# The first attention layer of a four-stage kernel with the operations of three batches in a new order on every engine

## The reference

```
x = x + gnn(layernorm(x), adj)                      # first stage
h = layernorm(x) @ W[head]                          # 512 x 64
weight[i,j] = leaky_relu(e_src[i] + e_dst[j], 0.01) # -1e9 where adj[i,j] == 0
attention = softmax(weight over j)
out = relu(attention @ h + bias) + h
gnn = layernorm over the 64 columns of out, * gamma + beta, heads side by side
```

## Time and profile before

| | us |
|---|---|
| median of 3 runs | 4832.03 |
| the profiled execution | 4839.06 |
| its span | 4837.3 |
| first score piece (DVE, line 847) starts | 43.69 |
| last one of the stage starts | 1216.75 |
| last operation of the stage (POOL, line 1053) starts | 1246.58 |

### The profile page before, as it was taken

The page is one execution under the profiler, slowest core; times in us unless marked ns, Lnnn a source line. Parts: engine busy times, 40 slices in busy tenths (PEclk is TensorE's granted clock), DMA queues, the critical chain, the costliest instruction groups (busy, mean ns, idle before and its releaser), DMA issues. The chain is left out here.

```text
span 4837.3 us, 142627 instructions
## 1 busy us (share of the span) xinstructions
PE 4119.1 (85%) x55809; PEld 2885.5 (60%) x55809; DVE 3534.2 (73%) x8962; ACT 2911.6 (60%) x7074; POOL 1201.2 (25%) x1028
## 2 busy tenths in 40 slices
PE   7888888888399999999998999975888888888882
PEld 4444444444156666666665788854777777777772
DVE  5888888888388888888887677753666666666666
ACT  5777777777298888888886666641333332333330
POOL 3666666665222222222222000000000000000000
PEclk9999999999699999999999999987999999999996
DMA  2121111111100000000001333331111111111115
GB/s 61 60 63 54 53 62 62 53 53 45 53 23 27 27 27 27 27 23 23 27 27 39 109 119 116 118 108 24 34 40 41 39 37 41 42 34 40 43 30 158
DMA packets 326283, 252.58 MB, mean 52 GB/s; under 512 B 171244, under 2 KB 289772, under 8 KB 323564
## 3 DMA queue, kind: packets, MB, share of 16 engines
q1 hardware_dynamic: 324076, 235.03, 16.8%
q10 hardware_dynamic: 1536, 8.39, 0.6%
HBM read 159.42 MB, written 67.11 MB: 47 GB/s over the span
## 5 line engine op out<-in xcount | busy, mean ns | idle before, releaser
L2309 PE MATMUL lstm_G_psum<-lstm_Whh,lstm_HT 128*32 128x192 f32 x8192 | 440.4, 333 | 268.1 <-DVE lstm_HT L2486 267.8
L847 DVE CUSTOM_DVE_ANT_0 g_S<-g_Z_psum,g_relu 128x512 f32<-128x512 f32 x640 | 438.3, 685 | 301.6 <-ACT g_relu L617 299.7
L617 ACT ACTIVATE g_relu<-g_Z_psum,g_src 128x512 f32<-128x512 f32 x640 | 436.8, 682 | 291.0 <-PE g_Z_psum L463 288.7
L2379 ACT ACTIVATE lstm_TC<-lstm_G_psum 128x192 f32<-128x192 f32 x512 | 170.9, 334 | 708.5 <-PE lstm_G_psum L2309 708.5
L473 PE MATMUL g_PT_psum<-g_ident,g_PR 128*128 128x128 f32 x2560 | 398.9, 279 | 158.3 <-DVE g_PT L855 92.3
L473 PEld LDWEIGHTS g_PT_psum<-g_ident,g_PR 128*128 128x128 f32 x2560 | 301.7, 142 | 354.1 <-ACT g_PR L651 237.2
L1785 ACT ACTIVATE ssm_EX<-ssm_Z_psum,ssm_tok 128x256 f32<-128x256 f32 (+1 forms) x1024 | 372.6, 424 | 155.1 <-PE ssm_Z_psum L1615 85.5
L651 ACT ACTIVATE g_PR<-g_S,g_nmax 128x512 f32<-128x512 f32 x640 | 456.9, 714 | 0.1
L2301 PE MATMUL lstm_G_psum<-lstm_Wih,lstm_XT 128*32 128x192 f32 x8192 | 428.0, 327 | 0.0
L2309 PEld LDWEIGHTS lstm_G_psum<-lstm_Whh,lstm_HT 128*32 128x32 f32 x8192 | 214.2, 109 | 355.2 <-DVE lstm_HT L2486 321.5
L2475 DVE SCALAR_TENSOR_TENSOR lstm_AB<-lstm_TC 128x128 f32<-128x128 f32 x512 | 150.2, 293 | 335.5 <-ACT lstm_TC L2379 331.5
(11 more groups left out here) (266 smaller groups left out, 10614.2 us busy)
## 6 DMA issues: line engine op xcount, KB each, us to landing
g_ADJ<-in_adj SPq DMA_DIRECT2D x64, 1024.0 KB, 5.6
x<-g_XO SPq DMA_DIRECT2D x64, 512.0 KB, 3.4
g_X<-in_x SPq DMA_DIRECT2D x32, 512.0 KB, 4.3
ssm_X<-x SPq DMA_DIRECT2D x32, 512.0 KB, 3.9
x<-ssm_OUT SPq DMA_DIRECT2D x32, 512.0 KB, 2.9
g_X<-x SPq DMA_DIRECT2D x32, 512.0 KB, 3.9
lstm_raw<-x SPq DMA_DIRECT2D x1024, 16.0 KB, 1.8
lstm_U<-x SPq DMA_DIRECT2D x128, 128.0 KB, 3.5
```

The lines of the kernel that those rows point to most:

```text
L617: act.activation(relu[n % 4][:, :], score_bank(b, n)[:, :], ACT.Relu, scale=(1.0 - ALPHA) / ALPHA, bias=src[b.slot][:, t, HH * p + hh:HH * ...
L847: v.tensor_tensor_reduce(S[n % 4][:, :], score_bank(b, n)[:, :], relu[n % 4][:, :], -1.0, 3e38, ALU.add, ALU.min, nmax[:, n % 4:n % 4 + 1] ...
L2309: ins = pe.matmul(bank[32 * j:32 * (j + 1), 0:last - first], HT[t % 2][:, 32 * kc:32 * (kc + 1)], Whh[:, kc, j, first:last], start=False, ...
```

## The change

`attention_phase(layer 0)` is replaced by a function of its own, `first_attention_phase`, which does the same operations on the same shapes. The order on each engine is no longer a loop over items but a list, `period(b)`, in which up to three batches stand beside each other, and the loop runs over periods. On DVE the list of period b has the work after the items of b-2, the items from 5 on of b-1, the first five items of b, and the statistics and first masks of b+1. `BANK` says which side bank each product uses, `DRAIN` what has read it, and `BEFORE` who had the bank before it in the list, and `bank_free` waits for that. The columns go to `Ab[1]` and stand before the projections; the outputs of the first pair of heads go to `Ab[0]`, those of the second to `Ab[1]` (both to `Ab[1]` before). POOL does the normalisation for b+2 first and the last step of the normalisation after the items one period later. `xt_out` also waits for both halves of the projections of the batch before, `relu_part` of item 0 waits for the first stage of `split` instead of the last, `h_out` also for `HB`, `load_x` also for `XN`. The statistics of batch 0 come after the preparations of the weights instead of before them.

The diff, cut to what is spoken of; of the lists of operations a few lines stand, their order shows below:

```diff
--- before.py
+++ after.py
@@ -1082,6 +1082,629 @@
+def first_attention_phase(nc, nb, x_in, adj, weights, consts, x_out, kept):
...
+    SLOTS = 3
+    NP = 2
+    ITEMS = 16
+    HH = 2
...
+        DRAIN = {"xnt0": (("xt", 2, 1),), "xnt1": (("xt", 2, 2),), "pj0": (("h", 2, 1),), "pj2": (("h", 2, 2),),
+                 "co0": (("s1", 1, 1),), "pt": (("rows", 1, 1),), "ob0": (("d1", 2, 1),), "ob1": (("d1", 2, 2),)}
+        BANK = {"xnt0": Ab[0], "xnt1": Ab[1], "pj0": Ab[0], "pj2": Ab[1], "co0": Ab[1], "pt": Ab[1], "ob0": Ab[0],
+                "ob1": Ab[1]}
+        BEFORE = {"xnt0": (("pj0", -1), ("ob0", -2),), "xnt1": (("pj2", -1), ("ob1", -2),), "pj0": (("xnt0", 0),),
+                  "pj2": (("pt", 0),), "co0": (("xnt1", 0),), "pt": (("co0", 0),), "ob0": (("pj0", 1), ("ob0", -1),),
+                  "ob1": (("pj2", 1), ("ob1", -1),)}
+        def bank_free(b, op):
+
+            for was, ago in BEFORE[op]:
+                if 0 <= (b + ago).off < nb:
+                    for sem, per, count in DRAIN[was]:
+                        (b + ago).wait(nc.tensor, s[sem], per, count)
...
+            def load_x(b):
+                if b.off == 0:
+                    return
+                b.wait(sp, s["xb"], 1, 1 - SLOTS)
+                b.wait(sp, s["xn"], IT, (1 - SLOTS) * IT)
+                sp.dma_start(X[b.slot][:, :, :], xv[b.index()]).then_inc(x_loaded[b.slot], 16)
+
+            def load_adj(b):
+                b.wait(sp, s["mask"], 1, 0)
+                b.wait(sp, s["check"], IT, 0)
+                sp.dma_start(ADJ[:, :, :], av[b.index()]).then_inc(s["adj_loaded"], 16)
+
+            def store(b):
+                b.wait(sp, s["out"], 1, 1)
+                sp.dma_start(ov[b.index()], XO[b.slot][:, :, :]).then_inc(stored[b.slot], 16)
+
+            def period(b):
+                at(b + 4, load_adj)
+                at(b + 5, load_x)
+                at(b, store)
+
+            for k in range(-5, nb + 0):
...
+            def xn_turned(b, kc):
+                b.wait(pe, s["xn"], IT, IT)
+                bank_free(b, f"xnt{kc}")
...
+            def columns(b, half_of):
+                b.wait(pe, s["xt"], 2, 2)
+                if half_of == 0:
+                    bank_free(b, "co0")
...
+            def outputs_turned(b, p):
+                b.wait(pe, s["ot"], NP, p + 1)
+                bank_free(b, f"ob{p}")
...
+            def period(b):
+                at(b, xn_turned, 0)
+                at(b + -1, scores, 9)
+                at(b + -1, turn, 6)
...
+            for k in range(0, nb + 1):
+                period(Batch(None, k, SLOTS))
...
+            def xt_out(b, kc):
+                b.wait(act, s["h_pe"], 2, 0)
+                b.wait(act, s["e_pe"], 1, 0)
+                b.wait(act, s["xt_pe"], 2, kc + 1)
...
+            def relu_part(b, n):
+                p, t, hh = item(n)
+                b.wait(act, s["z"], ITEMS, n + 1)
+                b.wait(act, s["s"], ITEMS, n - 3)
+                if n == 0:
+                    b.wait(act, s["s1"], 1, 1)
...
+                at(b, exp, 10)
+                at(b + -1, square)
...
+            def norm_stats(b):
+                b.dma_wait(v, x_loaded)
+                b.wait(v, s["xn"], IT, 0)
...
+            def normalise(b, p):
+                b.wait(v, s["ob"], NP, p + 1)
+                b.wait(v, s["rinv"], 1, 1)
+                b.wait(v, s["out"], 1, 0)
...
+                at(b + -2, residual)
+                at(b + -1, leaky, 9)
+                at(b + -2, residual_sum)
...
+            def period(b):
+                at(b + 2, normalised)
+                at(b + -1, layernorm, 3)
+                at(b + 1, bias_added)
+                at(b, centred)
+                at(b, residual)
+                at(b, layernorm, 0)
+                at(b, layernorm, 1)
+                at(b, layernorm, 2)
...
-        attention_phase(nc, 0, nb, a["x"], a["adj"], pick(GNN0), consts, x1, kept)
+        first_attention_phase(nc, nb, a["x"], a["adj"], pick(GNN0), consts, x1, kept)
```

476 lines of the change are left out of this document (added).

## The result

| | before | after |
|---|---|---|
| median, us | 4830.8 (4827.99 to 4834.06, 4 runs) | 4602.93 (4598.8 to 4605.82, 4 runs) |
| profiled execution, its span | 4839.06, 4837.3 | 4598.8, 4597.0 |
| last POOL operation of the stage ends | 1248.92 | 1015.04 |
| from there to the end of the span | 3588.4 | 3582.0 |

The ratio is 0.9527 (95% 0.9511 to 0.9544): 228 us less, where 152 were forecast and 4630 was the low end of the range. All of it is in the first stage (1248.92 less 1015.04 is 233.9); the later stages differ by 6.4, about the spread of the runs before (6.1).

The account below looks back on a forecast made before the run. A ring of waits bounds the kernel now, with no engine full; afterwards DVE's 32.3 us a period. 41.0 + 31 x 32.3 + 26 + 8.5 + 20.0 ends the stage at 1096.8, 152 earlier: 4680 us, range 4630 to 4760.

Parts of the forecast that it names:

- the low end of the range: Lowest total time the forecast range allowed: 4630 us, a first-stage period of T = 30.7 us.
- the DVE term: DVE's work per first-stage period, taken as 32.3 us with all four masks slow, and as the bound.
- The rule weighed there: Two-port VectorE operations and any GpSimd operation exclude each other for the whole instruction; so masks beside `XN` are slow.
- the rival "DVE falls to 29.3 to 30.3 and PE is the bound": First stage: masks beside `XN` are fast, PE sets T = 31.0 us, time 4640 us; chance 0.17.
- T: Period per batch in the first stage, forecast as 32.3 us and multiplied by 31 in the sum.
- tails: On PE, 0.16 us counted as busy ahead of each of some 8 waits a period, taken off its 31.40.
- The walk through the lists: DVE's list laid out over 32.3 us against the other engines: they come in time, so DVE runs without gaps.
- waits are left over: First stage: thin margins leave 2.2 us of the 5.3 us of gaps, T = 34.5, 4748 us; chance 0.25.
- no gain: First stage: the ring of waits re-forms elsewhere, T about 36.5 to 37.2, 4810 to 4832 us; chance 0.03.
- the chain over the load of `X`: Sum, centring, beta residual, load, statistics hold DVE: T = 37.2 to 37.5, 4832 to 4842 us; chance 0.05 (slower).
- The start: From weights' preparation to the first `leaky`: forecast at 41.0 us, 2.7 earlier than 43.69, with columns at 1.85.
- The square's stall: ACT's square waits 3.44 us for POOL, delaying a relu and DVE by 2.23 us; forecast to go.

Follow-up runs that it names:

- Experiment 5: Kernel before with only the four masks moved in DVE's list from items 4, 5, 6, 8 to 7, 8, 9, 12: 4827.01 us, ratio 0.9987.
- experiment 3: Kernel after without the product that adds the mask to the scores, 16 PE products fewer a batch: 4553.54 us, ratio 0.9432.
- experiment 1: Kernel after with a batch's four masks moved in DVE's list back towards POOL's large additions: 4616.49 us, ratio 0.9558.
- experiment 6: Kernel after with the first head pair's four weigh steps in two twos instead of one by one: 4602.67 us, ratio 0.9523.
- experiment 12: Kernel after with two more `bn_stats` a batch on DVE, 0.7 us of work that nobody reads: 4613.64 us, ratio 0.9545.
- experiment 4: Kernel before with ACT's square one item later and DVE's sum of squares in item 0 of the next batch: 4786.35 us, ratio 0.9911.
- 11: Kernel before with the first head pair's turned outputs in `Ab[0]` and the second's in `Ab[1]`, order unchanged: 4843.41 us, ratio 1.0020.
- Experiment 9: Kernel before with square and squares' sum later and the masks at items 7, 8, 9, 12: 4837.64 us, ratio 1.0008.
- experiment 10: Kernel before with square and squares' sum later and the masks at items 8, 9, 10, 12: 4794.69 us, ratio 0.9922.
- experiment 8: Kernel after with statistics and normalisation of batch 0 ahead of the weights' preparation: 4593.19 us, ratio 0.9501.

## Why the prediction was wrong in size and right in kind

The stage ends 82 us earlier than forecast (1015.04 against 1096.8). By the terms of the sum:

| term | forecast | measured | difference |
|---|---|---|---|
| first `leaky` | 41.0 | 42.17 | +1.2 |
| 31 distances from batch to batch | 31 x 32.3 = 1001.3 | 26.1 + 30 x 29.8 = 920.1 | -81.2 |
| last batch's 16 items | 26 | 25.9 | -0.1 |
| last `leaky` to the end | 28.5 | 26.9 | -1.6 |

- **The step that failed** is the DVE term: "With all four slow DVE has 32.3 us of work, with three fast 29.3. I take 32.3, by the nearest rows that are masks." All four are fast, and DVE's work is 28.6 us a period, 3.7 less. The two beside `XN`, which no row of before showed, run at full speed inside it; the timeline of the kernel after:

```profile
219.10 5.09 POOL L1653 TENSOR_SCALAR g_XN<-g_X,g_mv,g_rstd 128x256 f32<-128x256 f32 x4
...
223.54 0.41 DVE L1521 TENSOR_SCALAR g_MASK<-g_ADJ 128x512 bf16<-128x512 int32 x1
```
```profile
221.52 1.22 POOL L1653 TENSOR_SCALAR g_XN<-g_X,g_mv,g_rstd 128x256 f32<-128x256 f32 x1
...
222.72 1.47 POOL L1653 TENSOR_SCALAR g_XN<-g_X,g_mv,g_rstd 128x256 f32<-128x256 f32 x1
```

The last two lines are the third and the fourth of the four operations under `XN`: the fourth, into which both masks reach, takes 0.25 longer, so here POOL pays a little, and DVE 0.1 for one mask and nothing for the other. The mask beside the last normalisation (212.27, 0.42) falls beside an operation on 16 columns, and the one ahead of `bias_added` (228.13, 0.42) between two of POOL's. The nearest row was the slow mask beside an addition, but the cast inside `XN` was the row on the operation in question. Experiment 5 shows the same in the old order, with `XN` in both.
- The rule weighed there, the Trainium skill, "SBUF — State Buffer", section "Who interferes with whom", puts every operation of GpSimd in the same lock. The trace agrees for the two-input operations of 1024 columns (0.91, 2.22, 2.25 us) and not for the `XN` normalisation, whose masks took 0.41, 0.42 and 0.51, nor for the operation on 16 columns. The measurement decides: in the runs here only masks that meet a `TENSOR_TENSOR` of 1024 columns wait.
- The window of 36.70 us from which the sum took DVE's 31.34 and PE's 31.40 was short of a full period by 0.33. In the full 37.03 DVE is busy 31.67 and PE 31.74. With three masks 1.0 shorter that gives 28.7 for DVE, and 28.6 was measured.
- **The bound.** With fast masks the rival "DVE falls to 29.3 to 30.3 and PE is the bound" is what happened: PE is the fullest engine (29.64 of 29.80), and the period falls when products are taken from it (experiment 3). With DVE at 28.6 and ACT at 28.3 behind it the bound is not PE's alone, as experiments 1, 6 and 12 show. It was sized too high, T = 31.0: PE's work was put at 30.1 to 31.4 and is at most 29.64, and of the 0.9 us of waits that I added almost none is left. The 1.3 us of tails that I took off were too few: a full period of before has PE busy 31.74, 2.1 above what the same products take in the unbroken queue. And T stood for all 31 distances, but the first one, with no work of earlier batches in it, is 26.1 (33.98 against 37.03 before). So three terms were off in one direction, which is why even the low end (T = 30.7) did not hold the time: -75 us by the 30 full periods and -6 by the first.
- **The walk through the lists held.** Square with hardly a wait (forecast 0.4, none recorded), relus early, side banks and `X` in time: DVE's only waits a period are 0.6 for a turn and 0.3 for the outputs. The rival "waits are left over" is refuted (T 34.5), as are "no gain" and the chain over the load of `X`: its load is issued at 209.72, 5.9 after the sum, and the statistics start at 215.42, 5.7 later, with no recorded wait.
- **The start** is 1.2 later: the columns took 3.55 and not 1.85 us, and what follows them was 0.5 shorter than forecast. The last batch's items were met (25.9 against 26).
- Where the gain comes from: 7.2 us a period, 37.03 to 29.80, is the closing of gaps and the shorter masks. The square's stall alone gives 1.5 (experiment 4), masks alone 0.2 (5), banks alone less than nothing (11). Inside the whole order the places of the masks are worth 14 us, the bank 18, a wrong block of weigh steps 85. So the parts do not add up one by one: most of the gain belongs to the list as a whole. How it divides over its further moves was not tried.
- Experiment 9 lost its gain to the place of one slow mask and not to the clock (the windows of experiment 10). Why a mask at item 7 costs 1.5 us a period where three slow ones at items 4 to 6 cost nothing is not shown.

## What to carry to other kernels

Where no engine is full and the waits form a ring, lay the new list out against the fullest engine's work and trust the walk, but price each operation by the row beside the same neighbour, and carry the second-fullest engine through the sum with equal care: it becomes the bound. Single fixes in a ring of waits return little (43, 6 and -9 us here, of 228), and work taken off an engine that waits returns as waiting. Once an order is tight, 0.6 or 0.7 us more on an engine that has 1.2 to spare already shows (experiments 1 and 12), and any change of a neighbour's duration or place has to be timed.

## What the hardware did that was not expected

- A mask of DVE (128x512, int32 to bf16) that starts inside a POOL `TENSOR_TENSOR` of 1024 columns ends 0.28 us after it (330.67 + 0.91 against 331.30; 199.28 + 2.22 against 201.21 is 0.29), in the one case 0.63 us ahead of that end and in the other 1.93. Beside POOL's `TENSOR_SCALAR` of 256 columns it took 0.41 and 0.51, and POOL's operation 1.47 instead of 1.22.
- The columns took 3.55 us for 16 products at the start of the kernel after and 1.85 before, with a recorded granted clock of 1.00 (2.4 GHz) in both. They stood behind 1.76 us without products now, behind 6.77 us of unbroken ones before. In the kernel of experiment 8 they take 3.55 again, also behind 1.76. It is not the columns alone: the 8 projections right behind them took 3.76 in the kernel after, where 8 take 1.99 in the earlier trace rows, and before, the 16 projections ahead of the columns took 6.77. So PE worked at half its later pace for some microseconds, in both kernels, while the record says 1.00.
- Moving three masks by an item moved the mean granted clock of the stage from 0.94 to 0.97 in the old order (experiments 9 and 10); in the new one it is 1.00 in each window shown. A period of experiment 9 with a clock of 0.95 lasts as long as one with 1.00 (36.99), though PE is busy 1.6 us more in it.
